# Running both phase fronts of a channel block before its two accumulation tails, in a recurrent layer of a two-layer model

## The reference, cut to what matters

```python
x5   = x_val[..., None]                    # conv of xn @ W_in, one value per (t, head, h)
phi  = x5 * theta                          # 4 angles per value (M = 4)
poly = w[0] + w[1] * x5 - w[2] * x5**2
re_m, im_m = poly * cos(phi), poly * sin(phi)
p_w  = exp(clip(score * s_raw)) * time_w
cs   = cumsum([p_w * re_m, p_w * im_m, p_w], axis=1)      # over time
re, im = cs_re / den, cs_im / den
rsq  = rsqrt((sum(re**2) + sum(im**2)) / (2*H*M) + 1e-5)
y    = (re * rsq * ns) @ W_re + (im * rsq * ns) @ W_im
s    = (y * silu(gate)) @ W_out
```

## Time and profile before

| | |
|---|---|
| median of 3 runs | 6765.21 us |
| lowest and highest | 6760.71, 6774.36 us |
| profiled execution | 6765.04 us |
| its span on the slowest core (core 1) | 6763.4 us |
| spans of the eight cores | 6730.3 to 6763.4 us |
| mean granted TensorE clock, by core | 0.637 to 0.639 of full speed |

### The profile page before, as it was taken

The page is one execution under the profiler, slowest core; times in us unless marked ns, Lnnn a source line. Parts: engine busy times, 40 slices in busy tenths (PEclk is TensorE's granted clock), DMA queues, the critical chain, the costliest instruction groups (busy, mean ns, idle before and its releaser), DMA issues.

```text
span 6763.4 us, 35700 instructions; the slowest of 8 cores (6730.3 to 6763.4 us)
## 1 busy us (share of the span) xinstructions
PE 2581.7 (38%) x8358; PEld 826.6 (12%) x8358; DVE 2020.8 (30%) x4521; ACT 1271.6 (19%) x2230; POOL 188.2 (3%) x358
## 2 busy tenths in 40 slices
PE   0005322423422422104444655533444665555530
PEld 0001000100100100001111211111111211111110
DVE  8872463364266156221100100021222011111221
ACT  0001110111011011011100111103333244444300
POOL 0000000000000000000000011100000000000000
PEclk9997556655655655557777877765555755555575
DMA  2211102101200300334555444420000300000024
GB/s 51 47 39 16 15 0 45 24 0 17 52 0 1 61 6 0 69 84 59 82 77 75 85 66 66 67 40 2 1 1 1 47 5 5 5 5 5 8 52 132
DMA packets 271576, 239.39 MB, mean 35 GB/s; under 512 B 191826, under 2 KB 213970, under 8 KB 271346
## 3 DMA queue, kind: packets, MB, share of 16 engines
q0 software_dynamic: 52768, 116.50, 11.6%
q1 hardware_dynamic: 218610, 120.60, 8.5%
HBM read 284.17 MB, written 25.17 MB: 46 GB/s over the span
## 4 chain that ended last, share of the span: by engine, by line
DMA 29%; DVE 25%; PE 22%; ACT 12%; issue 9%; DVEq 2%; SPq 0%; ACTq 0%; POOLq 0%
DMA wstq<-l_wqkvT 7%; PE PS L2075 4%; ACT ptcol L2055 3%; PE PS L768 3%; DMA maskb<-masksf 3%; DVE csre L916 2%; PE PS L2044 2%; DVE csim L919 2%; DMA wfc<-l_win 2%; DMA wst<-l_wd 2%; ACT ptw L1848 2%; DMA wgu<-l_wg 2%; DMA wgu<-l_wu 2%; PE PS L1968 2%; DMA wfc<-l_wout 1%
## 5 line engine op out<-in xcount | busy, mean ns | idle before, releaser
L1656 PE MATMUL PS<-xnb_q,wstq 128*128 128x512 bf16 x1024 | 348.4, 503 | 286.4 <-DMA wstq<-l_wqkvT 249.3
L2055 ACT ACTIVATE ptcol<-PS,negmb 128x512 bf16<-128x512 f32 (+3 forms) x640 | 358.1, 625 | 466.7 <-PE PS L2044 466.7
L938 PE MATMUL PS<-sqt,psum 128*32 128x512 bf16 x128 | 76.4, 597 | 950.3 <-DVE sqt L932 950.3
L1532 PE MATMUL PS<-xnb,wgu 128*128 128x512 bf16 x1024 | 265.8, 426 | 320.0 <-DMA xnb<-xn 235.3
L2075 PE MATMUL PS<-ptcol,a 128*65 128x512 bf16 (+3 forms) x640 | 281.0, 557 | 236.5 <-ACT ptcol L2055 127.5
L2044 PE MATMUL PS<-xn_fm,g 64*128 64x512 bf16 (+3 forms) x640 | 277.3, 556 | 127.2 <-DMA A_fm<-outsb 126.8
L891 ACT ACTIVATE sinb<-frac 128x512 bf16<-128x512 f32 x128 | 73.7, 623 | 986.7 <-DVE frac L884 986.7
L768 PE MATMUL PS<-xn_fm,wfc 128*128 128x512 bf16 x512 | 221.2, 610 | 98.4 <-DMA wfc<-l_win 66.9
L549 PE MATMUL PS<-xq_fm,wqT 128*128 128x512 bf16 x256 | 57.9, 391 | 493.7 <-DMA wqT<-wq_st 493.7
L1711 DVE TENSOR_TENSOR qsl<-qsl,cosl 128x512 bf16<-128x512 bf16 x16 | 6.8, 426 | 721.6 <-DMA g<-ubuf 687.5
L1549 DVE TENSOR_TENSOR relub<-relub 128x512 bf16<-128x512 bf16 x64 | 27.2, 426 | 644.7 <-ACT ubuf L1544 644.7
(11 more groups left out here) (268 smaller groups left out, 4190.4 us busy)
## 6 DMA issues: line engine op xcount, KB each, us to landing
wstq<-l_wqkvT POOLq DMA_DIRECT2D x128, 256.0 KB, 4.1
wfc<-l_win POOLq DMA_DIRECT2D x64, 256.0 KB, 4.1
wgu<-l_wg POOLq DMA_DIRECT2D x32, 512.0 KB, 5.2
wgu<-l_wu POOLq DMA_DIRECT2D x32, 512.0 KB, 5.2
wst<-l_wd POOLq DMA_DIRECT2D x32, 512.0 KB, 5.3
xt<-x SPq DMA_DIRECT2D x16, 512.0 KB
wfc<-l_wout POOLq DMA_DIRECT2D x32, 256.0 KB, 4.0
xt_l<-x SPq DMA_DIRECT2D x16, 512.0 KB
```

Of the source, the lines that this page charges most:

```text
L1532: _h=hc: e.matmul(_b, _s, _m, start=(_h == 0), stop=(_h == 7)),
L1656: e.matmul(_b, _s, _m, start=(_d == 0), stop=(_d == 7)),
L2055: e.activation(ptcol[:, _o:_o + _w], PS[:, _o:_o + _w], AF.Exp, bias=negmb2[:, _h:_h + 1], scale=0.125), "act")
```

## The change

The half is split into two functions, `front(mp)` and `tail(mp)`, and a round now emits front 0, front 1, tail 0, tail 1. To let both fronts be in flight, `frac`, `sinb` and `cosb` get four buffers each, and the absolute value gets two tiles of its own (`afr`). Memory for it comes from three places: `pol2` is now the tile `pol1` (the product is written over its input), the debug part of `l32` is dropped, and the four `sqt` tiles are now `rein[0]`, `imin[0]`, `rein[1]`, `imin[1]`. Since PE reads `sqt`, tail 1 may no longer write `rein` and `imin` before the matmuls of tail 0 are done, so DVE's wait for `lastmm` moves from before the scans to before the products. ScalarE gets a wait for the previous front's cosines ahead of the absolute values, because both fronts share `afr`.

```diff
-    frac = [kb.S(f"frac{p}", (128, TC), F32) for p in range(2)]
-    afr = u_t
-    sinb = [kb.S(f"sinb{p}", (128, TC), BF16) for p in range(2)]
-    cosb = [kb.S(f"cosb{p}", (128, TC), BF16) for p in range(2)]
+    frac = [kb.S(f"frac{p}", (128, TC), F32) for p in range(4)]
+    afr = [kb.S(f"afr{p}", (128, TC), F32) for p in range(2)]
+    sinb = [kb.S(f"sinb{p}", (128, TC), BF16) for p in range(4)]
+    cosb = [kb.S(f"cosb{p}", (128, TC), BF16) for p in range(4)]
...
-    pol2 = kb.S("pol2", (128, TC), F32)
+    pol2 = pol1
...
-    sqt = [kb.S(f"sqt{p}", (128, TC), BF16) for p in range(4)]
+    sqt = [rein[0], imin[0], rein[1], imin[1]]
-    l32 = kb.S("l32", (32, 5 * TC), F32)
+    l32 = kb.S("l32", (32, (5 if want_dbg else 4) * TC), F32)
...
-            for mp in range(2):
+            def front(mp, prev_cos=None):
...
                 for p in range(2):
-                    op("scalar", lambda e, _p=p: e.activation(
-                        sinb[_p][:], frac[_p][:], AF.Sin, bias=0.0,
+                    op("scalar", lambda e, _q=2 * mp + p: e.activation(
+                        sinb[_q][:], frac[_q][:], AF.Sin, bias=0.0,
                         scale=float(2 * np.pi)))
+                if prev_cos is not None:
+                    kb.wait("scalar", "act", prev_cos)
...
+                return a_cos
+
+            def tail(mp, a_cos, lastmm):
+                ms = [2 * mp, 2 * mp + 1]
                 wait("vector", "act", a_cos)
+                if lastmm is not None:
+                    wait("vector", "te", lastmm)
                 for p in range(2):
...
                 wait("vector", "dve", g)
-                if lastmm is not None:
-                    wait("vector", "te", lastmm)
...
+            ac0 = front(0, prev_cos=prev_cos_c[0])
+            ac1 = front(1, prev_cos=ac0)
+            prev_cos_c[0] = ac1
+            lastmm = tail(0, ac0, lastmm)
+            lastmm = tail(1, ac1, lastmm)
```

More of the change, by code:

```diff
@@ L710, in emit_l0_attn @@
     rtmp = l32[0:32, 3 * TC:4 * TC]
-    rtmp2 = l32[0:32, 4 * TC:5 * TC]
+    rtmp2 = l32[0:32, 4 * TC:5 * TC] if want_dbg else None
     for (nm, tile) in (("l0_theta_r", thdiv), ("l0_wconv_r", wconv),
@@ L749, in emit_l0_attn @@
     sgadd_guard = [0, 0]
+    prev_cos_c = [None]
     for tc in range(NTC):
@@ L862, in emit_l0_attn @@
             drain("vector")
-            lastmm = None
-            for mp in range(2):
+            def front(mp, prev_cos=None):
                 ms = [2 * mp, 2 * mp + 1]
@@ L882, in emit_l0_attn @@
                     thc = thdiv[:, c * 4 + m:c * 4 + m + 1]
-                    g = op("vector", lambda e, _x=xvc, _th=thc, _p=p:
-                           e.scalar_tensor_tensor(
-                        out=frac[_p][:], in0=_x, scalar=_th, in1=k_r[_p][:],
+                    g = op("vector", lambda e, _x=xvc, _th=thc, _p=p,
+                           _q=2 * mp + p: e.scalar_tensor_tensor(
+                        out=frac[_q][:], in0=_x, scalar=_th, in1=k_r[_p][:],
                         op0=ALU.mult, op1=ALU.subtract),
@@ L890, in emit_l0_attn @@
                 for p in range(2):
-                    op("scalar", lambda e, _p=p: e.activation(
-                        sinb[_p][:], frac[_p][:], AF.Sin, bias=0.0,
+                    op("scalar", lambda e, _q=2 * mp + p: e.activation(
+                        sinb[_q][:], frac[_q][:], AF.Sin, bias=0.0,
                         scale=float(2 * np.pi)))
+                if prev_cos is not None:
+                    kb.wait("scalar", "act", prev_cos)
                 for p in range(2):
-                    ga = op("scalar", lambda e, _p=p: e.activation(
-                        afr[_p][:], frac[_p][:], AF.Abs, bias=0.0, scale=1.0),
+                    ga = op("scalar", lambda e, _p=p, _q=2 * mp + p:
+                            e.activation(
+                        afr[_p][:], frac[_q][:], AF.Abs, bias=0.0, scale=1.0),
                         "act" if p == 1 else None)
@@ L900, in emit_l0_attn @@
                 for p in range(2):
-                    a_cos = op("scalar", lambda e, _p=p: e.activation(
-                        cosb[_p][:], afr[_p][:], AF.Sin, bias=smalls[:, 4:5],
+                    a_cos = op("scalar", lambda e, _p=p, _q=2 * mp + p:
+                               e.activation(
+                        cosb[_q][:], afr[_p][:], AF.Sin, bias=smalls[:, 4:5],
                         scale=float(-2 * np.pi)), "act" if p == 1 else None)
+                return a_cos
+            def tail(mp, a_cos, lastmm):
+                ms = [2 * mp, 2 * mp + 1]
                 wait("vector", "act", a_cos)
+                if lastmm is not None:
+                    wait("vector", "te", lastmm)
                 for p in range(2):
[L906 to L909, removed]
+                    op("vector", lambda e, _p=p, _q=2 * mp + p: e.tensor_tensor(
+                        rein[_p][:], pp[:], cosb[_q][:], ALU.mult))
+                    g = op("vector", lambda e, _p=p, _q=2 * mp + p:
+                           e.tensor_tensor(
+                        imin[_p][:], pp[:], sinb[_q][:], ALU.mult),
                         "dve" if p == 1 else None)
                 wait("vector", "dve", g)
-                if lastmm is not None:
-                    wait("vector", "te", lastmm)
                 for p, m in enumerate(ms):
@@ L936, in emit_l0_attn @@
                 for p, m in enumerate(ms):
-                    op("tensor", lambda e, _c=c, _p=p, _st=(not msq_started):
+                    op("tensor", lambda e, _c=c, _p=p, _st=msq_st[0]:
                        e.matmul(pb[6][0:32, :],
@@ L940, in emit_l0_attn @@
                                 sqt[2 * _p][:], start=_st, stop=False), None)
-                    msq_started = True
+                    msq_st[0] = False
                     op("tensor", lambda e, _m=m, _p=p, _first=(m == 0):
@@ L954, in emit_l0_attn @@
                                          stop=(_m == 3)), "te")
+                return lastmm
+            msq_st = [not msq_started]
+            msq_started = True
+            lastmm = None
+            ac0 = front(0, prev_cos=prev_cos_c[0])
[3 more added lines that the diff above has]
+            lastmm = tail(1, ac1, lastmm)
             wait("vector", "te", lastmm)
```

## The result

The changed kernel takes 6689.99 us (median of 8 runs, 6681.08 to 6699.60) against 6771.80 us for the kernel before in the same comparison (8 runs, 6760.71 to 6791.55): ratio 0.9877, 95% interval 0.9863 to 0.9891. The forecast was 6687 us. The profiled execution has a span of 6691.5 us on its slowest core (core 3), 71.9 us less than before.

What follows compares the result with a forecast made beforehand. The prediction took a chain of waits, in the block loop DVE's instructions plus its gaps, as the bound. Per round 7.08 - 4.70 + 0.07 = 2.45 us, times 32 is 78.4 us off 6765.04: forecast 6687 us, range 6668 to 6708.

Steps and rivals of the forecast that it cites:

- The chain: Block loop: its time is DVE's instructions plus gaps waiting for cosines, matmuls and broadcast; summed gain 78.4 us.
- Front 1 leaves the chain: Each block-loop round: ACT's second cosines are hidden by tail 0, so all 7.08 us of front 1 go.
- The idle rest: Before tail 0: after both fronts on DVE, 0.56 us of idling for ACT remains each round.
- The wait that comes out: Between the tails: DVE's wait for tail 0's matmuls, formerly under front 1, is uncovered, 4.61 us a round.
- the prediction's sum: Each round: 7.08 - 4.70 + 0.07 = 2.45 us less; over 32 rounds 78.4 us.
- The place of the wait: Tail 1: waiting before the products instead of the scans costs 32 x 1.54 = 49 us, already within the 4.70.
- The waits on ACT: ACT's added wait on the previous front's cosines, in the fronts: taken at nothing, at most 6 us in all.
- Everything else at nothing: `pol2` over `pol1`, the dropped part of `l32`, tile memory, DMA and other stages: no effect on time.
- The rival clock: Block-loop matmul bursts run at the higher clock, each 1.97 us less, 126 us in all: 6561 us; chance 0.04.
- its mild form: Clock rises shortly before some matmul bursts end: some 15% of 126 us, 19 us, left in the range.
- The rival overlap: Block loop: ACT and DVE slow each other when overlapping; at twice their time 6886 us; chance 0.03.
- The rival absorbed: Something beside the chain bounds the time tile, so the gain is absorbed, near 6765 us; chance 0.04.

Runs made afterwards that it cites:

- The middle pair: Eight further matmuls in half 0's burst, in the changed kernel (6729.48 us, ratio 0.9948) and in the kernel before (6747.18 us, 0.9966).
- the third pair: 16 further matmuls in half 0's burst, in the changed kernel (6760.10 us, ratio 0.9982) and in the kernel before (6707.05 us, 0.9898).
- the doubled burst: Changed kernel with eight further matmuls of the same shape in half 0, into a bank nobody reads: 6729.48 us, ratio 0.9948.
- the four runs that took further waits out: Changed kernel with cumulative edits: squares in spent cosine tiles 0.9803, four csre/csim tiles each 0.9653, next round's fronts issued early 0.9437, next broadcast between bursts 0.9398.
- the next round's fronts under the last wait: Changed kernel with squares in cosine tiles and four csre/csim tiles each, plus next round's fronts issued before this round's last matmul wait: 6385.91 us, 0.9437.

## Why the prediction was right

- *The chain.* That the loop is DVE's instructions and waits held: the table of waits alone gives the 78.8 us, and 78.4 us were forecast. The medians differ by 81.8 us and the two profiled executions by 72 us. That the time itself was met within 3 us is in part luck: the forecast started from 6765.0 us, 6.8 us below the median of the larger sample, and its gain was 3.4 us short of the measured one.
- *Front 1 leaves the chain, 7.08 us.* Right: `u_t` to `rein` is 7.09 us with both fronts in it. The idle rest is 0.63 us, not 0.56, because DVE's instructions overlap between the fronts too; it changes nothing, since ACT ends that stretch.
- *The wait that comes out, 4.61 us.* Right, 4.57 us on average. It grew to 6.63 and 8.61 us with longer bursts and vanished with tiles of its own, and the time followed each time. By the prediction's sum a round gains 7.08 + 0.07 - 0.09 less this wait; over 32 rounds that is 80, 14 and -50 us for the three bursts. Measured, as the median of the order of before less that of the changed order: 82, 18 and -53 us. The middle pair's intervals overlap; the other two are clear. (In the third pair the small waits beside this one nearly cancel: 6.2 us of the scans in the order of before, and 4.4 us of `y_u` and 2.5 us of `pwx` more in the changed order.)
- *The place of the wait, 49 us.* Right: 53 us when it was moved back.
- *The waits on ACT, at nothing.* Right: ACT's three pairs take the same time from start to start as before.
- *Everything else at nothing.* Right: with the order undone the ratio is 1.0002.
- *The rival clock.* In most bursts of eight matmuls it did not occur, as forecast, but its mild form did, "a clock that rises shortly before some bursts end". Of the 64 waits for a burst in the changed kernel 50 are 4.61 or 4.62 us long; 14 are 0.15 to 0.44 us shorter, 4 us in all of the 19 us that the range had left for it. They come in pairs, the last burst of one round and the first of the next. In one of them the last two of eight matmuls run at the higher level:

```profile
866.75 0.61 PE L952 MATMUL PS<-csre,wy 128*128 128x512 bf16 x1
867.29 0.40 PE L956 MATMUL PS<-imin,psum 128*32 128x512 bf16 x1
867.62 0.39 PE L960 MATMUL PS<-csim,wy 128*128 128x512 bf16 x1
```

  The kernel before has such waits too (12 of its 32 are below 4.60 us), so the prediction's statement that its bursts run at 0.50 held for the round shown and not for all. With 16 matmuls the rise came within the burst, and the expectation of the doubled burst had left it out.
- *The rival overlap.* Refuted: 748 and 715 ns before, 749 and 715 ns after, 748 and 714 ns with full overlap. The Trainium skill ("SBUF — State Buffer", Who interferes with whom) names only the port pair that DVE shares with GpSimd as a place of contention between engines; the trace agrees for these forms.
- *The rival absorbed.* Refuted: the time went on falling with the loop in the four runs that took further waits out.

Left open is how the program's size shortens the weight loads. That it moves the program and the tensors to other places in memory was only argued, and no run tells that from the fetching of instructions. Nor is size the whole of it: in one kernel without further matmuls (the next round's fronts under the last wait) core 3 had loads of 3.9 us and a stage of 592 us, cores 1, 5 and 7 had 4.1 us and 619 to 621 us, and even cores of several kernels took 599 to 607 us with loads of 3.9 or 4.0 us. Only the 564 to 577 us of the four kernels with 512 further matmuls lie below everything that was seen without them.

## What to carry to other kernels

Hoisting work out from between two waits takes away a stall and uncovers whatever that work had covered: subtract the wait that comes next, and look for the size at which it turns the sign (here a wait of 7.06 us by the sum, between the measured cases of 6.63 us, still a gain, and 8.61 us, a loss). Memory saved by sharing a tile with one that another engine still reads is paid for by an earlier wait; share with a tile whose last reader is the engine that writes it next. Undo the order alone to see whether a gain is the order's, and when an edit adds or drops many instructions, compare the stages that it does not touch.

## What the runs showed of the hardware

- A burst of eight matmuls with these gaps ran at 1.2 GHz to its end (0.54 us each) in 50 of 64 cases of the changed kernel; in the others the clock rose before its end. In a burst of 16 it rose within the burst in every round (waits of 5.96 to 7.36 us), and its end ran at 0.32 us each.
- DVE's and ACT's forms of 128x512 took the same time alone and beside each other: 748 ns for `frac` and 714 to 716 ns for `cosb`.
- A 256 KB weight load of layer 1 landed in a median of 4.1, 3.9 to 4.0 and 3.6 us in kernels with 0, 256 and 512 further matmuls (cores 1, 3, 5 and 7; one core with none had 3.9), wherever the 512 stood and however small they were; the stage took 613 to 624 us (that one core 592), 600 to 607 and 564 to 577 us.
